# Linear attention between two gated feed-forward blocks on one Trainium2 core: the attention chunk in a new order, with its outputs behind the second block of queries

## The reference, cut to what matters

```python
x = x + 0.5 * _L0_ffn_ref(_layernorm(x), ...)       # gated, ternary weights, hidden 512
x = x + _L0_attn_ref(_layernorm(x), ...)            # linear attention, 16 heads of 64, and a GELU block
x = x + 0.5 * _L0_ffn_ref(_layernorm(x), ...)       # the first block again
...
def _linear_attention(x, Wq, Wk, Wv, Wo):
    Q = _phi(x @ Wq); K = _phi(x @ Wk); V = x @ Wv  # _phi(x) = elu(x) + 1, heads of 64
    KV = jnp.einsum('bhti,bhtj->bhtij', K, V)
    S = jnp.cumsum(KV, axis=2)                      # causal: the state up to each token
    z = jnp.cumsum(K, axis=2)
    num = jnp.einsum('bhti,bhtij->bhtj', Q, S)
    den = jnp.maximum(jnp.einsum('bhti,bhti->bht', Q, z), EPS_DEN)[..., None]
    return (num / den) @ Wo
```

## Time and profile before

| | before |
|---|---|
| median of 3 runs | 857.38 us (855.78 to 858.56) |
| the profiled execution | 863.09 us |
| its span, first to last instruction | 861.4 us |
| busy: TensorE, VectorE, ScalarE, GpSimd | 798.1, 558.9, 563.2, 364.7 us |
| mean granted TensorE clock | 0.990 of 2.4 GHz |

### The profile page before, as it was taken

The page is one execution under the profiler, slowest core; times in us unless marked ns, Lnnn a source line. Parts: engine busy times, 40 slices in busy tenths (PEclk is TensorE's granted clock), DMA queues, the critical chain, the costliest instruction groups (busy, mean ns, idle before and its releaser), DMA issues. The chain is left out here.

```text
span 861.4 us, 26994 instructions
## 1 busy us (share of the span) xinstructions
PE 798.1 (93%) x11458; PEld 676.0 (78%) x11458; DVE 558.9 (65%) x1290; ACT 563.2 (65%) x1024; POOL 364.7 (42%) x292
## 2 busy tenths in 40 slices
PE   1799999998899999999999999998989899999997
PEld 0688888877788888879889888887777678888886
DVE  7655564374866878677687876878777582818120
ACT  3687777757655555646556755555668477777774
POOL 4597979682100101010010100101266487979784
PEclk9999999999999999999999999999999899999999
DMA  7001120201001001010010101101023320201010
GB/s 256 0 25 56 44 64 10 79 8 49 16 3 39 16 4 52 3 40 16 3 52 3 42 14 39 53 4 40 27 81 95 96 60 13 62 12 50 1 50 26
DMA packets 56762, 34.55 MB, mean 40 GB/s; under 512 B 1984, under 2 KB 55232, under 8 KB 56640
## 3 DMA queue, kind: packets, MB, share of 16 engines
q1 hardware_dynamic: 56640, 32.79, 13.2%
HBM read 22.29 MB, written 10.49 MB: 38 GB/s over the span
## 5 line engine op out<-in xcount | busy, mean ns | idle before, releaser
L1157 ACT ACTIVATE ee<-ps 128x512 f32<-128x512 f32 x128 | 77.8, 608 | 89.2 <-PE ps L821 62.3
L1776 POOL TENSOR_TENSOR axs<-ay,axr 128x512 f32<-128x512 f32 x8 | 10.2, 1273 | 275.9 <-DVE ay L1572 275.9
L1659 POOL TENSOR_TENSOR alA<-full,ahA 128x512 fp32r<-128x512 f32 x74 | 100.0, 1366 | 42.6 <-DVE ahA L1324 35.7
L676 PE MATMUL ps<-ahA,wh 128*128 128x512 f32 x288 | 114.6, 398 | 1.4 <-POOL alA L1659 1.4
L1316 DVE SCALAR_TENSOR_TENSOR full<-ps,sc,gate 128x512 f32<-128x512 f32 x64 | 46.6, 747 | 106.5 <-PE ps L676 66.0
L676 PE MATMUL ps<-ahB,wh 128*128 128x512 f32 x288 | 113.3, 393 | 0.0
L676 PE MATMUL ps<-alA,wh 128*128 128x512 f32 x288 | 113.3, 393 | 0.0
L676 PE MATMUL ps<-alB,wh 128*128 128x512 f32 x288 | 112.2, 390 | 0.0
L1659 POOL TENSOR_TENSOR alB<-full,ahB 128x512 fp32r<-128x512 f32 x76 | 98.8, 1313 | 14.2 <-ACT ahB L1065 8.6
L1064 ACT ACTIVATE full<-ps,sc 128x512 f32<-128x512 f32 x86 | 59.5, 692 | 34.2 <-PE ps L676 24.4
L1158 ACT ACTIVATE rr<-ps 128x512 f32<-128x512 f32 x128 | 78.0, 609 | 0.0
(11 more groups left out here) (179 smaller groups left out, 2274.5 us busy)
## 6 DMA issues: line engine op xcount, KB each, us to landing
wst<-in_ternary SPq DMA_DIRECT2D x5, 512.0 KB, 8.2
stage<-in_attn SPq DMA_DIRECT2D x4, 512.0 KB, 4.9
xlnA<-x_scratch SPq DMA_DIRECT2D x8, 256.0 KB, 3.3
axr<-x_scratch SPq DMA_DIRECT2D x8, 256.0 KB, 3.3
yx_scratch<-ay SPq DMA_DIRECT2D x8, 256.0 KB, 2.3
xs_scratch<-axs SPq DMA_DIRECT2D x8, 256.0 KB, 2.4
xlnA<-yx_scratch SPq DMA_DIRECT2D x8, 256.0 KB, 3.2
xlnB<-yx_scratch SPq DMA_DIRECT2D x8, 256.0 KB, 3.4
```

Source lines behind the costliest of these rows:

```text
L676: ins = nc.tensor.matmul(b[:, :], w[:, col(k):col(k) + P], x_[:, k, :], start=(k == 0 and j == 0), stop=(k == ks[-1] and j == terms - 1))
L1157: nc.scalar.activation(ee[k][:, :], src[:, :], ACT.Exp).then_inc(*X["act"].step(f"e_{name}"))
L1659: return nc.gpsimd.tensor_tensor(dst, src, hi.bitcast(F32), ALU.subtract)
L1776: nc.gpsimd.tensor_tensor(axs[:, :, :], ay[:, :, :], axr[:, :, :], ALU.add).then_inc(*X["pool"].step(f"ys{i}"))
```

## The change

No instruction is added or removed; the attention's work is put into another order.

- TensorE: D and S of chunk `g` no longer end the chunk before but stand behind K{n}.1, in chunk g itself. `outputs(g)` moves behind the second block of queries, so that Q, V and Q stand ahead of it and one V behind it. WO of a half tile moves from the end of the odd chunk into the next even chunk, between S and the first Q. `nT` now follows OT directly.
- VectorE: `accumulated(g)` and `masked(g)` stand between the two `phi` of K. `divided(g)` and `once` come behind both `phi` of Q, and `twice` follows directly.
- ScalarE: only WO's copy moves. In the last two chunks the products of the GELU block, their activations and the norms are reordered too, and behind them `residual(7)` goes ahead of `f_normalise(4)` on VectorE. GpSimd's and SyncE's orders stay.
- The banks of the ring are dealt in the new order, which changes who waits for whom.

```diff
@@ attention_pe: TensorE's loop @@
-                state_products(0)
-                scores(0)
                 for g in range(NC):
...
                     if more:
                         for h in range(2):
                             token_major("K", n, h)
-                    else:
-                        f_first(0, (0, 1))
-                    outputs(g)
+                    state_products(g)
+                    scores(g)
+                    if not more:
+                        f_first(0, range(KT))
+                    if g and c % 2 == 0:
+                        projected(hh - 1)
                     for j in range(2):
                         if hh + 1 < NHALF:
                             queries(hh + 1, 2 * (g % 2) + j)
+                        if j:
+                            outputs(g)
                         if more:
                             token_major("V", n, j)
-                        if c == 0 and i and j == 0:
-                            back(i - 1)
+                    if c == 0 and i:
+                        back(i - 1)
...
                     transposed_outputs(g)
...
-                    if more:
-                        state_products(n)
-                        scores(n)
...
-                    if g % 2:
-                        after("dve", f"ol{g}.1")
-                        three(bank(f"WO{hh}")[:, 0:2 * P], ...
-                        if hh + 2 < NHALF:
-                            norm(hh + 2)
+                    if g % 2 and hh + 2 < NHALF:
+                        norm(hh + 2)
+                f_last(0)
+                projected(NHALF - 1)
@@ attention_dve: VectorE's loop @@
                     if more:
-                        for h in range(2):
-                            phi(f"K{n}.{h}")
+                        phi(f"K{n}.0")
+                    accumulated(g)
+                    masked(g)
+                    if more:
+                        phi(f"K{n}.1")
...
-                    for j in range(2):
-                        divided(g, j)
-                    if c == 1 and i + 1 < NT:
-                        once(i + 1)
                     for j in range(2):
                         if hh + 1 < NHALF:
                             phi(f"Q{hh + 1}.{2 * (g % 2) + j}")
-                        if c == 0 and i and j == 0:
-                            residual(i - 1)
+                        if j:
+                            for k in range(2):
+                                divided(g, k)
+                            if c == 1 and i + 1 < NT:
+                                once(i + 1)
+                    if c == 0 and i:
+                        residual(i - 1)
                     if c == 1 and i + 1 < NT:
                         twice(i + 1)
...
                     for j in range(2):
                         low_outputs(g, j)
-                    if more:
-                        accumulated(n)
-                        masked(n)
@@ ffn_dve, behind the attention @@
                 for t in range(2, NT):
-                    f_normalise(t + 2)
                     if t == 2:
                         residual(NT - 1)
+                    f_normalise(t + 2)
```

More of the change, by code:

```diff
@@ L426, in attention_plan @@
             kt((0, 1), 0)
-            state_products(0)
-            scores((6, 7), 0)
+            for bank in (0, 1):
+                turn()
             for g in range(NC):
-                c, i, n, hh, old = g % Q, g // Q, g + 1, g // 2, g % CB
+                c, i, n, hh = g % Q, g // Q, g + 1, g // 2
                 more, queries = n < NC, hh + 1 < NHALF
@@ L463, in attention_plan @@
                 else:
[L464 to L467, removed]
+                    tail(6, "N2", "act_fn", "hi", 2)
+                    for m in range(KT):
+                        tail((1, 0, 3, 4)[m], f"L1.{m}", "act_f1", ("hi0", "hi1", "full2", "hi3")[m], 1)
                 for j in range(2):
@@ L920, in transposed_outputs, with projected @@
                     transposes(bank(f"OT{g}.{j}"), [ot[:, 2 * p:2 * p + 2, :] for p in range(4 * j, 4 * j + 4)], X["pe"], f"OT{g}.{j}")
+            def projected(hh):
+                after("dve", f"ol{2 * hh + 1}.1")
+                three(bank(f"WO{hh}")[:, 0:2 * P],
+                      [(wah[:, 3 * DA + p * P:3 * DA + (p + 1) * P], wal[:, 3 * DA + p * P:3 * DA + (p + 1) * P],
+                        oh[:, p, :], ol[:, p, :]) for p in range(PR)], f"WO{hh}")
             def back(i):
@@ L1193, in attention_first, with projected @@
                     norm(hh)
+            def projected(hh):
+                h = hh % 2
+                after("pe", f"WO{hh}")
+                if h == 0 and hh:
+                    after("pe", f"yT{hh // 2 - 1}")
+                nc.scalar.copy(ayf[:, h * 2 * P:(h + 1) * 2 * P], ps[X["banks"].bank[f"WO{hh}"]][:, 0:2 * P])\
+                    .then_inc(*X["act"].step(f"wf{hh}"))
             def attention_act():
@@ L1208, in attention_act @@
                             exp_relu(f"K{n}.{h}")
+                    else:
+                        f_gelu(0, range(KT))
+                    if g and g % 2 == 0:
+                        projected(hh - 1)
                     for j in range(2):
@@ L1231, in attention_act @@
                         f_norm(1)
[L1232 to L1241, removed]
-                        nc.scalar.copy(ayf[:, h * 2 * P:(h + 1) * 2 * P], ps[X["banks"].bank[f"WO{hh}"]][:, 0:2 * P])\
-                            .then_inc(*X["act"].step(f"wf{hh}"))
-                        if hh + 2 < NHALF:
-                            norm(hh + 2)
+                    if g % 2 and hh + 2 < NHALF:
+                        norm(hh + 2)
+                f_evacuate(0)
+                projected(NHALF - 1)
             tern_act(ffn1, attention_first)
```

83 lines of the change are left out of this document (42 added, 41 removed).

## The result

The changed kernel took **875.5 us** (median of 4 runs, 873.6 to 875.7). The kernel before, on the same chip, took 856.7 (4 runs, 855.8 to 858.6). The ratio is 1.021 [1.019, 1.024]: slower by 18.8 us. The forecast was 866.8 us in a range of 855 to 877.

A forecast was written before the change was run, and what follows sets the result against it. The prediction took TensorE as the bound, busy 798.1 of 861.4 us. Terms 16.8 - 4.6 - 5.2 + 3.4 - 1.0 = +9.4 us took the profiled 863.1 to 872.5; less 5.7 to the median, 866.8 us, range 855 to 877.

The forecast's parts named there:

- The wait for `axn`: Before `nT` in seven c = 1 chunks: TensorE waits 2.4 us each, +16.8 us, 10.9 to 22.4.
- the chain's 1.56: Lower bound per c = 1 chunk: VectorE's path to `axn` 6.29 us minus TensorE's path to OT's end 4.73.
- being late: VectorE behind in c = 1 chunks: 0.3 us of waiting and 0.5 of lateness, making the wait 2.4 us.
- signs of being wrong: `axn` waited for under 1.6 us a chunk, score gaps vanishing or doubling, or new waits in chunks with c other than 1.
- WO's wait: WO's first product in the attention no longer waits for VectorE; 3.1 and 1.5 us go, -4.6 us.
- The "issue" gaps: In the scores, 10.4 us of unexplained TensorE waits; half come back as K's products let the queue fill, -5.2 us.
- The clock: TensorE at half clock after two of the seven new attention waits: +3.4 us, bounds 0 to 12.
- The ends: Attention's start and GELU block: two waits lose their cause, two or three new ones appear; -1 us, -4.2 to +3.
- The base: Sum added to the profiled execution's 863.1 us, then 5.7 taken off because the median was 857.4.
- "Faster": VectorE not late into c = 1 chunks, `axn` wait stays at 1.56 us: about -3, 854 us; chance 0.15.
- "Even": `axn` wait as forecast, but all score gaps go and the clock holds: +0.8, 858 us; chance 0.12.
- "The clock falls each time": Half clock behind all seven `axn` waits, 12 us in place of 3.4: +18.0, 875 us; chance 0.12.

The follow-up runs named there:

- the second trace: The kernel before, profiled once more with no edit: one run, 858.07 us, span 856.4 us.
- experiment 10: The changed kernel with 128 always-satisfied waits (64 more TensorE instructions when compiled) ahead of the attention's products: 880.1 us, ratio 1.025.
- experiment 7: The changed kernel with only `f_stats(3)` moved ahead of the last two `ol` on VectorE: 867.7 us, ratio 1.010.
- experiments 4 and 5: 4: changed kernel, `f_normalise(4)` ahead of `residual(7)` again, 874.6 us, ratio 1.018. 5: kernel before, `residual(7)` ahead of `f_normalise(4)`, 858.9 us, ratio 1.0005.
- edits 2 and 3 together: The changed kernel with `axn` transposes behind the next chunk's keys and `once` ahead of the second queries' `phi`: 857.7 us, ratio 0.9975.

## Why the prediction was right in its direction, and small in its size

The kernel is slower, as forecast, and by the mechanism that carried most of the sum. The size is 18.8 us in place of 9.4. The terms (us), against both traces of the kernel before:

| term | forecast | against the first | against the second |
|---|---|---|---|
| waits for `axn` and for the second queries' bank | +16.8 | +12.9 | +12.9 |
| VectorE's other results, WO's above all | -4.6 | -5.0 | -5.9 |
| "issue" gaps | -5.2 | -1.8 | -1.4 |
| TensorE's busy time in the attention (the clock) | +3.4 | +3.2 | +4.8 |
| small waits not listed | 0 | +0.8 | +0.9 |
| behind the outputs of chunk 28 | -1.0 | +2.0 | +5.7 |
| ahead of those of chunk 0 | 0 | -1.6 | -1.5 |
| sum | +9.4 | +10.5 | +15.5 |

The sum of the first trace agrees with the forecast only because its errors cancel: the waits were taken 3.9 us too large, the gaps and the ends together 6.4 too low, and the 1.6 us gained ahead were not foreseen. That is luck, and so is it that 875.5 us lies in the range, 1.5 under its top: the top stood there for a clock that falls behind every wait, and it didn't.

**The wait for `axn`: mechanism right, size too large.** Taken 2.4 us a chunk, 16.8 in all, with 0.3 of it as a wait for the second queries' bank. Measured 10.4 for `axn`, 1.06 to 1.84 us each, and 2.5 for that bank (`am`, in five of the seven chunks and in no other, mostly 0.42). Where no instruction gap disturbs the chunk the two make 1.83 + 0.42 = 2.25 us, close to what was walked: the chain's 1.56, and 0.7 in place of 0.8 for being late. What the walk missed is that in four of seven chunks a gap stands in O: in three TensorE lost that time anyway and waited less for `axn`, in the fourth the divisions, which need O, were pushed back too. So the total is 12.9 in place of 16.8; seven undisturbed chunks would make 15.8. One of the prediction's own signs of being wrong, `axn` waited for in under 1.6 us a chunk, did appear: three of the seven waits are 1.06 to 1.09 us, and the mean is 1.49.

**WO's wait: right.** -4.6 was forecast for `ol` and `middle`. Against the second trace of before 3.3 + 2.3 + 0.9 = 6.5 us of waits for VectorE are gone in the attention; 0.4 for `ol` and 0.2 for `ot` are left.

**The "issue" gaps: half was forecast to come back, -5.2; about -1.4 came** (in the stretch between chunk 0's and 28's outputs 10.8 in the second trace of before, 9.4 after). The reason given for a gain, that K's long products let the queue fill, is not what decides: the gaps sit at the block borders, and the order only decides what stands there. The sentence of the Trainium skill weighed there ("Runtime: NRT & Kernel Launch", Instruction fetch mechanics, the cost of a border is mostly hidden) fits 56 of the 67 borders counted in experiment 10, those in 64-wide products mostly too, but not the 11 others, 10 of them in S or O; the longest gap in any of these traces is 2.2 us.

**The clock: +3.4 was taken, for two of seven waits.** In the attention one of seven fell, to 0.50 for 3.40 us at 554.1, at most 1.7 us. The first trace of before has as much at 383.2, so against that one the clock costs nothing there. The 2.09 us that the prediction calls a gap still held 16 products; the gap in it is 1.88 us, and one of 1.80 at 264.0 in the same trace had no half clock behind it.

**The ends: the step that was missed.** Taken at -1, with +3 as the worst; measured +5.7 against the second trace (278.3 - 272.6), +2.0 against the first. The prediction named the cause, `f_stats(3)` behind the last `ol`, but priced it at about 1 us and gave the clock nothing there. The rows of VectorE, GpSimd and TensorE show it:

```profile
635.79 1.29 DVE L1565 TENSOR_TENSOR ol<-ps,oh 128x512 fp32r<-128x512 f32 x2 [4.10 <-ACT oh L1241]
636.99 0.86 DVE L1275 BATCH_NORM_STATS2 bstB<-xlnB 128x6 f32<-128x128 f32 x4
...
639.60 3.02 DVE L1288 TENSOR_SCALAR xnB<-xlnB,bagB,rsB 128x128 f32<-128x128 f32 x4 [1.12 <-POOL rsB L1727]
639.53 1.27 POOL L1664 TENSOR_TENSOR nlA<-stage,nhA 128x512 fp32r<-128x512 f32 x1
640.76 1.26 POOL L1664 TENSOR_TENSOR ahB<-full,ahB 128x512 fp32r<-128x512 f32 x1
642.67 1.01 PE L649 MATMUL ps<-ident,xnB 128*128 128x128 f32 x4 [2.41 <-DVE xnB L1288]
```

VectorE stands idle for 4.10 us ahead of `ol`, and the statistics that it could have done in that time come behind it; `xnB` ends at 642.6, and TensorE waited 2.41 us for it. Lateness is not all of it: `xnB` takes 3.02 us here, beside GpSimd's two subtractions, and 1.11 us in experiment 7, at 636.21, where those were over at 635.9. What the prediction expected to gain, `ay` and part of `xnA`, did go, but by experiments 4 and 5 the swap that removes `ay` brings no measurable time. New are 1.6 us more for `nhA`, 1.0 for `am` and 0.9 for the `ol` ahead of S. In all TensorE waits only 1.1 us more in this part than in the second trace. The rest is busy time, 259.0 us in place of 254.4: the half clock behind the wait for `xnB` (3.35 us) and at 690.6 (6.83) accounts for it. The second of the two isn't the change's alone, since the first trace of before has the same 6.8 us at 680.1. Experiment 7 takes one instruction group out of that place and gets nearly all of it back; the price of these statistics is shown, how much of it is clock differs from run to run.

**The base.** The sum was made against an execution 5.7 us above the median, and the same 5.7 taken off again. Its excess was mostly half clock behind the attention, which the changed kernel has too, though it had been no part of the median of before. The forecast missed by 8.7 us: 1.1 between the profiled executions (872.5 and 873.6), the 5.7 taken off, and 1.9 by which the traced execution of after lies under its median. So the largest step of the miss is this correction, and not a term of the sum.

Of the 4.8 us more busy time in the attention, half clock is at most 1.7. The first product of each `wah,ahh` group took 3.5 us more in all (mean 450 instead of 419 ns), and 2.9 of that is V's first product where it stands right behind O: 28 times 0.50 us, where the same product in the middle of a run takes 0.39 to 0.40. Before, a Q stood there, and the Q groups' first products (`ahh,wah`) lost 1.5 us. With edits 2 and 3 together V's is still 0.50 us, while the busy time of the attention is back at 345.9 us (345.4 before). So this one comes from the order and not from VectorE being late. What else grew, and went again with both edits, I didn't separate.

**The rivals.** "Faster" fell: its condition, a wait at its lower bound or under it, came about in three of the seven chunks, but the gaps did not come back. "Even" fell with the gaps as well. "The clock falls each time" gave 875 us, and that is what was measured, by another road: the clock fell once in the attention, and the rest lay at the end and in the base.

## What to carry to other kernels

Where a small chain runs over two engines (here statistics, a root on GpSimd and a scaling), its first part belongs ahead of work that covers the other engine's latency; giving that cover back took 9 us out of the attention. A new order for the engine that bounds the kernel can be slower until the helpers' orders are fitted to it: here the same TensorE order lay at +2.1% with one VectorE order and at +0.1% with two moves on VectorE; a third move, on TensorE too, brought -0.8%. And trace the kernel before twice before adding terms to one execution: the two traces here gave +2.0 and +5.7 us for the same part.

## What the hardware showed that I had not expected

- TensorE stops at some borders of its instruction blocks: between 213 and 600 us at 11 of 67 in the changed kernel, for 0.5 to 1.4 us from one start to the next, and for up to 2.4 us in the other traces. The place in a count by 256 is the same each time, and 64 instructions more ahead move them in the code. Each of these pauses ended 2.2 to 3.1 us after a fetch of 16 KB had started.
- 64 satisfied wait instructions in a row took some 6 us, about 0.1 us each; the mean granted clock there was 0.69.
- A wait of about 2 us was sometimes followed by half clock and sometimes not: one of the seven waits of 1.1 to 1.8 us for `axn`; in the two traces of the kernel before the gap behind the same 56 scores was 1.88 us with half clock behind it once, and 1.82 us with full clock the other time; and of six traces with the wait of 2.4 us for `xnB` four have 3.4 us of half clock right behind it.
- VectorE's `xnB`, four instructions of 128x128, took 3.02 us with GpSimd's subtractions beside it and 1.11 us without them.
